# Value matmuls moved into the middle of the next unit's stretch, with three probability buffers and half-sized q/k split staging, in a fused adaLN attention and mixture FFN kernel

## The reference

```python
mod = (silu(c) @ wmod).reshape(8, 6, 1, 256)         # sa, ca, ga, sb, cb, gb
h = layernorm(x) * (1 + ca) + sa
q, k, v = (lora_linear(h, w, a, b) for ...)          # x @ w.T + (x @ a.T @ b.T) / 16
scores = q @ k^T / 4, causal mask; attn = softmax(scores)
x = x + ga * lora_linear(attn @ v, wo, ao, bo)
h = layernorm(x) * (1 + cb) + sb
# top-2 of 4 experts, each relu(h @ Wi.T + (h @ A_e.T) @ B_e.T) @ Wo.T, weighted
x = x + gb * ffn(h)
```

## Time and profile before

| what | before |
| --- | --- |
| runs, median of 3 | 2151.95 us (2151.85 to 2155.94) |
| span of the profiled execution | 2145.5 us |
| PE busy | 1892.0 us (88%) |
| DVE busy | 1199.8 us (56%) |
| ACT busy | 938.8 us (44%) |
| POOL busy | 529.7 us (25%) |
| bytes moved by DMA | 111.82 MB |

### The profile page before, as it was taken

The page is one execution under the profiler, slowest core; times in us unless marked ns, Lnnn a source line. Parts: engine busy times, 40 slices in busy tenths (PEclk is TensorE's granted clock), DMA queues, the critical chain, the costliest instruction groups (busy, mean ns, idle before and its releaser), DMA issues.

```text
span 2145.5 us, 36829 instructions
## 1 busy us (share of the span) xinstructions
PE 1892.0 (88%) x11124; PEld 980.5 (46%) x11124; DVE 1199.8 (56%) x2697; ACT 938.8 (44%) x1701; POOL 529.7 (25%) x823
## 2 busy tenths in 40 slices
PE   8687888999889989899889998899898998798858
PEld 5233343455435454354534555354543545344435
DVE  3755567555665557655575556655576554755132
ACT  2254444544444544544444444444445443544421
POOL 3111122322222212223223222222122232132223
PEclk9889989999999999999999999999999999999979
DMA  5523333121433222232331214332222323210100
GB/s 170 80 50 60 60 57 78 22 63 23 80 60 67 33 39 77 31 70 32 65 79 20 62 24 81 60 67 33 36 70 41 70 31 65 31 26 16 35 0 20
DMA packets 72349, 111.82 MB, mean 52 GB/s; under 512 B 13940, under 2 KB 41680, under 8 KB 72152
## 3 DMA queue, kind: packets, MB, share of 16 engines
q1 hardware_dynamic: 72136, 109.31, 27.3%
q10 hardware_dynamic: 16, 0.02, 0.0%
HBM read 75.20 MB, written 33.57 MB: 51 GB/s over the span
## 4 chain that ended last, share of the span: by engine, by line
PE 61%; DVE 14%; DMA 8%; issue 7%; SPq 5%; ACT 4%; POOL 0%; DVEq 0%; POOLq 0%; ACTq 0%
PE mxs L747 11%; PE ov L776 9%; PE st L761 9%; PE dense L856 8%; DMA k_st<-k_parts_scratch 8%; PE dense L841 5%; DVE negm L1147 4%; PE dense L867 4%; PE dense L791 4%; SPq L577 4%; PE dense L833 3%; PE dense L733 3%; PE mxs L751 2%; SPq L581 1%; DVE stats L1018 1%
## 5 line engine op out<-in xcount | busy, mean ns | idle before, releaser
L915 ACT ACTIVATE probs<-st 128x512 f32<-128x512 f32 (+1 forms) x1216 | 666.9, 576 | 651.2 <-PE st L761 613.2
L747 PE MATMUL mxs<-k_st,q_st 96*128 96x512 bf16 (+3 forms) x1536 | 463.4, 333 | 54.6 <-DMA k_st<-k_parts_scratch 48.2
L1147 DVE TENSOR_REDUCE negm<-mxs 128x1 f32<-128x512 f32 (+4 forms) x736 | 416.1, 613 | 147.8 <-PE mxs L751 147.4
L761 PE MATMUL st<-q_st,k_st 98*128 98x512 bf16 (+3 forms) x1536 | 453.0, 335 | 38.9 <-issue 24.3
L1147 DVE TENSOR_REDUCE negm_left<-mxs 128x1 f32<-128x512 f32 x512 | 330.0, 684 | 168.0 <-PE mxs L747 165.5
L776 PE MATMUL ov<-probs,v_g 128*32 128x512 f32 (+3 forms) x3072 | 333.5, 506 | 22.7 <-POOL probs L634 21.9
L747 PEld LDWEIGHTS mxs<-k_st,q_st 96*128 96x128 bf16 x1536 | 149.0, 98 | 333.9 <-issue 101.7
L856 PE MATMUL dense<-c_t,wi_t 128*128 128x512 f32 x512 | 247.3, 605 | 4.3 <-ACT ratio_b L965 3.7
L631 POOL TENSOR_TENSOR fence<-fence 128x1 f32<-128x1 f32 x256 | 49.9, 195 | 756.8 <-ACT probs L915 756.6
L761 PEld LDWEIGHTS st<-q_st,k_st 98*128 98x128 bf16 x1536 | 140.1, 99 | 202.6 <-issue 76.3
L655 POOL TENSOR_TENSOR hid<-hid,second 128x512 f32<-128x512 f32 x128 | 159.8, 1270 | 245.1 <-DVE second L1211 244.6
(11 more groups left out here) (162 smaller groups left out, 1715.3 us busy)
## 6 DMA issues: line engine op xcount, KB each, us to landing
q_st<-q_parts_scratch SPq DMA_DIRECT2D x192, 128.0 KB, 6.9
k_st<-k_parts_scratch SPq DMA_DIRECT2D x192, 128.0 KB, 7.4
q_parts_scratch<-q_part SPq DMA_DIRECT2D x16, 768.0 KB, 3.3
k_parts_scratch<-k_part SPq DMA_DIRECT2D x16, 768.0 KB, 5.4
xin<-in_L_attn_x SPq DMA_DIRECT2D x9, 1024.0 KB, 5.1
x<-in_L_attn_x SPq DMA_DIRECT2D x8, 1024.0 KB, 10.6
out_x<-ob SPq DMA_DIRECT2D x64, 128.0 KB, 1.7
q_st<-m_row SPq DMA_DIRECT2D x128, 4.0 KB
```

The costliest lines, as they stand in the source:

```text
L747: last = nc.tensor.matmul(mxs[:, bank_m, j * n:(j + 1) * n], q_st[0:KS, slot, h0 + j, qt * P:(qt + 1) * P], k_st[0:KS, slot, h0 + j, k0:k0 ...
L761: last = nc.tensor.matmul(st[:, score_bank(ch, kt, h0), j * n:(j + 1) * n], k_st[0:KS + 2, slot, h0 + j, kt * P:(kt + 1) * P], q_st[0:KS + ...
L915: nc.scalar.activation(probs[:, par, h0:h0 + heads, 0:n], st[:, score_bank(ch, kt, h0), 0:heads * n].rearrange("p (j q) -> p j q", q=n), A ...
L1147: nc.vector.tensor_reduce(dst[:, h0:h0 + heads], src, axis=AX.X, op=ALU.max, negate=True).then_inc(max_free, 1)
```

## The change

The value matmuls of unit u-1 are issued at turn 0.5 of stretch u, and not at the end of stretch u-1. What follows `pv` follows it: the copy of `ov`, and `ce`, which stands in stretches 5 and 1 (it was 4 and 0). At a batch's start `ct` goes from stretch 0 to 1 and `op` from 1 to 2. Since a unit's probabilities live longer, `probs` gets three buffers. The memory for it comes from `q_part` and `k_part`, which hold one half `ot` and not both, so that ACT's write into them waits for the stores of both halves so far. The setup data that lay in these tensors move to other ones.

```diff
@@ body_plan
-    if post:
-        put(0, ("ce", GROUPS - 1, 1))
     if pre:
         put(0, ("ls1",))
     if post:
-        put(0, *[("ct", i) for i in range(4)])
+        put(1, ("ce", GROUPS - 1, 1), *[("ct", i) for i in range(4)])
     if pre:
         put(1, ("ln1",))
     if post:
-        put(1, *[("op", i) for i in range(4)])
+        put(2, *[("op", i) for i in range(4)])
...
-        if k in (4, 0) and u > 0:
-            pinned.append(("ce", g, 0) if k == 4 else ("ce", g - 1, 1))
+        if k in (5, 1) and u > 1:
+            pinned.append(("ce", g, 0) if k == 5 else ("ce", g - 1, 1))
...
+        if u or post:
+            turns.append((0.5, 3, ("pv", (u - 1) // NU % 2, *UNITS[k - 1])))
         for _, n, s in sorted(turns, key=lambda turn: turn[:2]):
             plan.append(s)
...
+            if n == 3 and UNITS[k - 1][1] == 4 * UNITS[k - 1][0] + 3:
+                plan.append(("ov", UNITS[k - 1][0]))
...
-        plan.append(("pv", g % 2, c, kt))
-        if kt == 4 * c + 3:
-            plan.append(("ov", c))
@@ buffers
-        q_part = sb("q_part", [P, 2, 3, S], BF16)
-        k_part = sb("k_part", [P, 2, 3, S], BF16)
+        q_part = sb("q_part", [P, 3, S], BF16)
+        k_part = sb("k_part", [P, 3, S], BF16)
-        probs = sb("probs", [P, 2, HG, HB])
+        probs = sb("probs", [P, PROBS, HG, HB])
@@ ACT, pj
-                    after(act, parts_out[ot], done(f"ps{ot}") * (2 * 16))
+                    for stored in range(2):
+                        after(act, parts_out[stored], done(f"ps{stored}") * (2 * 16))
@@ DVE, vg
-                    after(dve, pv_done, done("pv") - VG_UNIT - 1)
+                    after(dve, pv_done, done("pv") - VG_UNIT)
```

More of the change, by code:

```diff
@@ L61 @@
 VG_UNIT = 8
+PROBS = 3
 V_FREE = (GROUPS - 2) * NU + VG_UNIT + 1
@@ L235, in epilogue_plan @@
 def epilogue_plan():
-    plan = [("xl",), ("ce", GROUPS - 1, 1)] + [("ct", i) for i in range(4)] + [("op", i) for i in range(4)]
+    plan = [("pv", (GROUPS - 1) % 2, *UNITS[-1]), ("ov", 1), ("xl",), ("ce", GROUPS - 1, 1)] + [("ct", i) for i in range(4)] + [("op", i) for i in range(4)]
     plan += [("ls2",), ("ln2",)] + [("t2", i) for i in range(4)] + [("rt",), ("rx",), ("ro",)]
@@ L425, in adaln_block @@
         a_pad = probs_f[:, KC * 6 * D:KC * 6 * D + 4 * D].rearrange("p (m d) -> p m d", m=4)
[L426 to L429, removed]
+        w_raw = c_t[:, :, :].rearrange("p k n -> p (k n)").rearrange("p (m t d) -> p m t d", m=4, t=KC)
+        bt_pad = x1[:, 0:4, :]
+        kp_f = k_part[:, :, :].rearrange("p a b -> p (a b)").bitcast(F32)
         b_raw = kp_f[:, 0:128].rearrange("p (m t r) -> p m t r", m=4, t=KC)
@@ L435, in adaln_block @@
         eb_w = low_st[:, 1, 0:FT * KS].rearrange("p (t s n) -> p t s n", t=FT, s=SPLIT)
[L436 to L440, removed]
+        c_raw = kp_f[:, 256:512]
+        c_sig = kp_f[:, 512:768]
+        c_sil = kp_f[:, 768:1024]
+        cond_t = kp_f[:, 128:128 + KC * NB].rearrange("p (k b) -> p k b", k=KC)
+        gate_raw = kp_f[:, 1024:1024 + 2 * D]
         gate_abs = o_sb[:, 0, :]
@@ L626, in run @@
                     if kt // 4 == ch and h0 + heads == HG:
-                        par = UNITS.index((ch, kt)) % 2
+                        par = UNITS.index((ch, kt)) % PROBS
                         pool.wait_ge(exp_done, done("qk") + 1)
@@ L638, in run @@
                     which, ot, half = a
-                    dst = (q_part if which == "q" else k_part)[:, ot, :, half * HB:(half + 1) * HB]
+                    dst = (q_part if which == "q" else k_part)[:, :, half * HB:(half + 1) * HB]
                     par = 0 if which == "q" else 1
```

2 lines of the change are left out of this document (1 added, 1 removed).

## The result

Before and after were run in turn on the same chip. The kernel before took 2152.48 us (median of 4 runs, 2151.85 to 2155.94), the changed one 2301.03 us (4 runs, 2299.16 to 2303.16). The ratio is 1.0688, with a 95% interval of 1.0673 to 1.0703: 149 us slower. The direction was as forecast and the size was not: 2301 lies above the whole range.

A forecast was written before the change was run, and what follows sets the result against it. PE was taken to bound the kernel from a group's first maximum to its last, with DVE and transfers holding the ends. Terms of 26, 14, 21, 16, 16 and 1 sum to 94 us: 2246 us, forecast's range 2210 to 2265, 8-in-10 range 2186 to 2276.

The forecast's parts named there:

- The pins: At group ends DVE's reductions hold `nm` and the last transfer holds the first maximum; from there to `nm` PE limits.
- their signs: Transfer waits well over 100 us, `nm` waits about 1.7 each, POOL mask waits gone, low clock behind a batch's first maxima.
- terms 1, 2, 3 and 5: Between first maximum and next `nm`: an extra unit 26 us, `ce` 14, batch starts 21, low clock 16.
- terms 4 and 6: At group ends, before the first maximum: transfers start later, 16 us; ACT's write waits for the half-sized staging's stores, 1 us.
- Term 5: Behind first maxima, low clock after longer PE idling: 1.5 us at seven jumps, 0.9 at six first-group ends; 16 us, bounds 0 to 44.
- Terms 1 and 4: One more 512-wide unit behind the first maxima, 26 us; at group ends, transfers start later behind (1, 4), 16 us.
- term 1: Between first maximum and next `nm`, one more 512-wide unit: 1.0 us in 24 loop phases, 0.3 in seven others; 26 us.
- term 4: At group ends stores and transfers start later: 1.0 us at first-group ends and loop jumps, 0.2 at 19 others; 16 us.
- Terms 2 and 3: `ce`, and at seven batch starts the four `ct`, move from under the transfer wait to behind the first maximum: 14 and 21 us.
- term 2: `ce` moves between first maximum and next `nm`, delaying the next instruction about 0.5 us, 28 times: 14 us.
- Terms 6 and 7: ACT's write into half-sized `q_part` and `k_part` waits for stores, 1 us in all; the third probability buffer alone, nothing.

The follow-up runs named there:

- one_unit_late: Order of the kernel before with the changed kernel's memory, but value matmuls of unit (1, 6) alone moved to the middle of the next stretch: 2156.50 us, ratio 1.0029.
- after_unrolled: The changed kernel with the loop's six iterations written out, so without a jump: 2289.74 us, ratio 1.0645 to the kernel before.
- warm_all: The changed kernel plus unused matmuls, 15 ahead of `t2` and 20 ahead of every group's first maxima: 2315.23 us, ratio 1.0757 to the kernel before.
- inner_mid: Order of before, changed kernel's memory; value matmuls of units (0, 1) to (1, 3) and the first half's copy and `ce` moved mid next stretch: 2191.47 us, ratio 1.0179.
- nm_back: The changed kernel with only the value matmuls of unit (1, 4) put back ahead of `nm`: 2268.12 us, ratio 1.0537 to the kernel before.
- ce_back: The changed kernel with `ce`, `ct` and `op` in their old stretches and (1, 7)'s value matmuls at the next stretch's start: 2269.68 us, ratio 1.0562.
- mem_old_order: The changed kernel's three buffers and half-sized staging, with every step in the order of the kernel before: 2147.52 us, ratio 0.9994.

## Why the prediction failed in its size

**The pins and their signs were right.** `nm` waits 1.53 in place of 0.74 us, 49.0 us in all; the wait for POOL went and gave nothing (one_unit_late); low clock stands behind the first maxima. The wait for the transfers came to 80.1 and not well over 100 us, because PE now arrives later at the jump, by the second stop. In after_unrolled, which has no jump, it was 125.4. An iteration grew by 21.4 us, in place of the 12 to 14 forecast.

**Where the sum went wrong.** Between the pins the forecast had 77 us (terms 1, 2, 3 and 5), and 141 were measured; under them 17 (terms 4 and 6), and 7 were measured. Two things between the pins make up most of what is missing, the clock and the place in mid-stretch.

**Term 5, the clock (16 us, bounds 0 and 44), is the term that was most mis-sized.** I let only the long waits at 13 places lower the clock, at 1.5 and 0.9 us each. Between the pins PE is busy at the low clock for 94.8 us more, which costs 47 us; warm_all got 48 back. The upper bound fell short too, since it allowed 1.7 us per pin: behind the jump 7 us of low clock follow, which cost 3.5. PE's idle time at the jump, which I had at 4.92 and 6 us, was right in sum (10.1). The Trainium skill, TensorE: Matmul & The Clock Gate, section "HAM oscillation — how this bites in real kernels", has a kernel whose bursts start cold after each wait. The trace stands nearer to that than I weighed it, but not wholly on its side. Nine of the loop's twelve ordinary groups are at full clock throughout behind waits of 1.1 to 1.6 us, as the one shown above at 729.18:

```profile
729.18 0.38 PE L726 MATMUL mxs<-k_st,q_st 96*128 96x512 bf16 x1 [1.07 <-DMA k_st<-k_parts_scratch]
```

**The middle of a stretch was priced at nothing, without a word.** The prediction counted eight units for seven and took their new places inside the stretches as equal to the old. inner_mid shows 41 us for it, 36 of them in its profile between the pins. Some 13 us are idle time, most of it maxima that wait for a bank, and some 10 low clock. Some 14 us are busy time that the clock does not explain, and their cause stays open. No term covered any of this.

**Terms 1 and 4, the two units that cross a pin (26 and 16 us).** Put back, they are worth 60 us. Their own price stands in ordinary groups without low clock: 38.04 to 36.94 us, 1.1 each, as term 1 had it for the loop, and 34 us if all 31 pay it. Much of the remainder is clock: low clock between the pins falls from 127.6 to 59.8 us with both back. The two units are paid in different places, (0, 0) between the pins, and (1, 4) under them, as a delay of what the transfers wait for (23 us in nm_back, in place of the 16 of term 4).

**Terms 2 and 3, `ce` and `ct` (14 and 21 us).** 19 us on the rung that takes them out, where (1, 7) moves too, and 27 us in ce_back: below the 35 forecast. In an ordinary group `ce` costs 0.36 us where term 2 has 0.5. Between the pins alone they cost more, 51 us on that rung, and 36 came back under them.

**The jump.** The forecast took its stop of 4.92 us over from rows 6. With the last unit's value matmuls behind it there are two stops. Unrolling says that this is worth 18 us of the difference at most. Most of these are low clock, which between the pins fell from 127.6 to 105.3 us in the changed kernel and rose from 27.9 to 56.0 in the kernel before. Why it rose there is open.

**Terms 6 and 7, the staging and the third buffer (1 and 0 us), held.** mem_old_order shows it for the old order. In the new one ACT's 7.00 us and PE's 4.87 us stand ahead of a first maximum that still waits 1.96 us for transfers. SP issued these as quickly as before (8.2 us from the store to the last of the twelve at 920.17, before 8.5), so the two waits lie in their shadow. The new order with the old staging could not be tried: with three buffers it has no room, and with two a unit's exponentials overwrite one that is still being read.

## What to carry to other kernels

Before moving work off a place where it "costs an idle engine nothing", ask three things: does it go from under a wait with a fixed end to a stretch that the engine itself limits; does the idle time that it leaves behind lower TensorE's clock for the stretch that follows; and does it cross a loop's jump. Here the first two cost 20 us or more each and the third at most 18, and the wait that the change removed was worth nothing. Price a new order as well as new counts: the same work in the middle of the next stretch, instead of the end of its own, was the largest single rung.

## What the runs showed of the hardware that was not expected

Leaving out 96 transposes made the kernel 6 to 7 us slower and PE 11.4 us busier. Matmuls of no use in PE's waits, twenty ahead of each burst of maxima, took the low clock behind them away (127.6 to 21.4 us between the pins). At a loop's jump PE stopped once for 4.5 to 5.1 us (the kernel before), or twice for 2.8 to 3.2 and 5.7 to 7.2 us (the changed one), with instruction transfers in the trace but nothing that the profile names as the releaser. Writing the loop out made one kernel 9 us faster and the other 9 us slower.
